# A convolutional LSTM ahead of an attention and experts block: the gates computed by one sigmoid, the skip split between ScalarE and GpSimd

## The chip, the cores and the metric

The kernel runs on one core of a Trainium2 chip. The metric is the device time of one execution in microseconds, by its median over the runs shown.

## The reference, cut to what matters

The input x is (16 samples, 96 channels, 16 rows, 16 columns). First comes a recurrent layer that walks over the 16 image rows, then an attention layer with six heads, then a feed-forward layer with four experts, all in float32. Only the recurrence is touched by the change. With the masked convolution of x shuffled into four gates of 48 channels, `h_rows`, it is:

```
def step(carry, h_row):
    _h, c = carry
    s = conv1d(_h, w1, width 3, padded) + h_row
    o, f, i, g = jnp.split(jax.nn.sigmoid(s), 4, axis=1)
    c = f * c + i * g
    _h = o * jnp.tanh(c)
    return ((_h, c), _h)
_, out_h = lax.scan(step, init, h_rows)
return x + conv1x1(out_h, w_skip * mask) + b_skip
```

Here `init` is zero, the convolution over `_h` runs along the 16 columns of a row, and the result, read as 256 tokens of 96 channels per sample, goes into the attention.

## The kernel before, in words

**Engines.** The program is written engine by engine, each with an order of its own, joined by semaphores. TensorE multiplies, VectorE (DVE), ScalarE (ACT) and GpSimd (POOL) compute, SyncE (SP) issues most transfers.

**Recurrence.** A row of the image is done in two half-steps, one for samples 0 to 7 and one for samples 8 to 15, so there are 32 half-steps m, each of 128 columns (8 samples by 16 positions). Half-step m depends on half-step m − 2. The four gates stand in one PSUM bank as two column blocks c = 0, 1 on 112 partitions: one gate of a block on partitions 0 to 47, the other on 64 to 111. Before: o and f in block 0, i and g in block 1. Four banks rotate as G[q].

In the order of one half-step: `input_part` (L857) puts the masked convolution of x into the bank, four matmuls over 96 partitions, two half-steps ahead. `state_part` (L870) adds the three taps over h: `wsa_sb` contracts over 112 partitions, since `h_pad` holds h on partitions 0 to 47 and once more, shifted by one column, on 64 to 111; `wsb_sb` adds the last tap. `skip` (L880) multiplies the h of half-step m − 2 with the skip weights into bank K. A 128-column float32 matmul is two records in the trace, each with its own weight load.

ACT takes tanh of half the gates (L466 for f and g, L467 for o and i), since sigmoid(x) = (1 + tanh(x/2))/2. VectorE works with these doubled values: `cell` (L620) with five instructions (L623 to L631), `cell_h` (L633) with the two writes of h (L641, L642), `add_skip` (L644) with one (L649) that adds skip, bias and x into `t_cm`. The factors 1/2 are put into the weights once, at L599 to L601. ACT's third instruction of a half-step is the tanh of c (L471). TensorE waits for h (`h_ready`), for a free bank (`gates_tanh`) and for the skip's bank (`t_half`). GpSimd has no work in this part but to clear buffers.

**Start.** SP issues w_input, the first two rows of x, w_state, two more rows, b_skip, the rest of x, then the other weights. VectorE waits for w_input (L594) and masks it (L596); TensorE then does four input parts. VectorE waits for w_state and b_skip (L598).

**End of the recurrence and what follows.** The last two skips wait for the last h; `keep_clock` (L909) issues small matmuls that nobody reads between the waits. With all of `t_cm` written (`t_half` = 32), TensorE transposes the first tokens (L928). Eight blocks of 512 tokens follow: layer norm, q, k and v, scores (L968 to L973), exponentials on ACT (L518) with the division on GpSimd (L406), transposes of the probabilities (L984), values (L1005, four or three matmuls with 32 output columns each, at different column groups), the output projection (L1011), the experts' first layer (L1042 to L1046) with Gelu, the routing (L753 is its last step on VectorE) and the experts' second layer (L1022, which adds the bias by a matmul with two contraction rows, then L1026).

## Time and profile before

| | us |
|---|---|
| median of 3 runs | 467.11 (464.62 to 467.35) |
| profiled execution, its own time | 466.77 |
| its span, first to last instruction | 465.0 |
| TensorE matmuls busy | 435.8 (94%) |
| VectorE busy | 269.5 (58%) |
| ScalarE busy | 263.6 (57%) |
| GpSimd busy | 145.8 (31%) |

The span is the profiled execution from its first to its last instruction; its own time holds what lies around that too. Busy time of TensorE is an upper figure, because matmuls are pipelined and their ends are modelled: the distance between the starts of two matmuls is the better measure of what one costs. In a timeline row, "x8" is eight records merged, the second number is the time that they span, and square brackets hold the idle time of the engine before them and what ended it.

### The profile page before, as it was taken

Reading aid. Unit: us, or ns where it says so; the run is one execution under the profiler, and the core shown is the slowest. Engines: PE = TensorE matmul, PEld = TensorE weight load, DVE = VectorE, ACT = ScalarE, POOL = GpSimd, SP = SyncE. Lnnn points to the kernel's source line nnn. Section 1 sums busy time; section 2 is a strip of 40 time slices with the busy share of each in tenths; the row PEclk is TensorE's granted clock in tenths of the full one; section 3 lists DMA queues with packets and bytes.
Section 4 is the critical chain, followed back from the end, with each engine's and each line's share of the span. In section 5 each row is a group of like instructions: output and inputs, shape, how many; then the busy total and the mean of one; then the engine's idle time right before and its main releaser. Section 6 shows DMA issues by size and latency. Waiting matters only on the chain.

```text
span 465.0 us, 10797 instructions
## 1 busy us (share of the span) xinstructions
PE 435.8 (94%) x3199; PEld 347.0 (75%) x3199; DVE 269.5 (58%) x954; ACT 263.6 (57%) x740; POOL 145.8 (31%) x309
## 2 busy tenths in 40 slices
PE   6999998759899999999999999999999999999897
PEld 6999996436568777877777778678767877787676
DVE  3888888535525852775277437634763585266424
ACT  2544454336477648664865585567657764865370
POOL 5000000425422542362255315531542254235200
PEclk9999999997999999999999999999999999999999
DMA  8600000021021002101210120022002100200000
GB/s 200 134 0 0 0 0 1 25 68 27 1 61 28 19 15 67 39 0 37 52 30 0 45 51 22 0 51 51 17 0 59 42 0 13 68 22 1 15 4 18
DMA packets 14393, 14.95 MB, mean 32 GB/s; under 512 B 5426, under 2 KB 11412, under 8 KB 14372
## 3 DMA queue, kind: packets, MB, share of 16 engines
q1 hardware_dynamic: 14180, 14.30, 12.3%
q0 software_dynamic: 192, 0.39, 0.3%
q8 instruction: 10, 0.16, 0.1%
q14 instruction: 11, 0.09, 0.1%
HBM read 3.86 MB, written 1.57 MB: 12 GB/s over the span
## 4 chain that ended last, share of the span: by engine, by line
PE 74%; DVE 12%; ACT 5%; issue 5%; SPq 2%; DMA 1%; POOL 1%; DVEq 1%; ACTq 0%; POOLq 0%
PE F L1026 19%; PE T L984 9%; PE A L1005 8%; PE F L1042 4%; PE S L968 4%; PE F L1046 4%; PE F L1043 3%; PE S L970 3%; PE F L1022 3%; PE S L973 2%; DVE c L629 2%; DVE ig L627 2%; ACT tc_sb L471 2%; DVE pt_sb L457 1%; PE M L947 1%
## 5 line engine op out<-in xcount | busy, mean ns | idle before, releaser
L406 POOL TENSOR_SCALAR p_sb<-p_sb,rden 128x128 f32<-128x128 f32 (+1 forms) x192 | 79.3, 427 | 133.4 <-DVE rden L710 131.2
L1026 PE MATMUL F<-w_sb,hid 128*128 128x96 f32 x768 | 101.0, 276 | 0.0
L1026 PEld LDWEIGHTS F<-w_sb,hid 128*128 128x128 f32 x768 | 93.4, 192 | 5.9 <-issue 5.9
L518 ACT ACTIVATE p_sb<-S,nmax 128x128 f32<-128x128 f32 (+1 forms) x192 | 78.8, 425 | 17.4 <-DVE nmax L704 17.3
L704 DVE TENSOR_REDUCE nmax<-S 128x2 f32<-128x512 f32 (+1 forms) x80 | 50.7, 634 | 53.1 <-PE S L973 52.8
L457 ACT COPY pt_sb<-T 128x512 f32<-128x512 f32 (+1 forms) x48 | 26.4, 550 | 69.2 <-PE T L984 69.2
L564 ACT ACTIVATE hid<-F,b_sb 128x512 f32<-128x512 f32 x72 | 49.3, 686 | 8.2 <-PE F L1046 7.5
L1005 PE MATMUL A<-pt_sb,v_cur 128*32 128x128 f32 x576 | 44.2, 284 | 8.4 <-ACT pt_sb L457 4.5
L984 PE MATMUL T<-id_sb,p_sb 128*128 128x128 f32 x288 | 49.3, 290 | 1.4 <-POOL p_sb L406 1.4
L968 PE MATMUL S<-k_bd,q_st 96*128 96x384 f32 (+2 forms) x96 | 38.7, 410 | 4.8 <-DMA k_bd<-k_cur 3.8
L984 PEld LDWEIGHTS T<-id_sb,p_sb 128*128 128x128 f32 x288 | 30.9, 143 | 16.2 <-issue 14.1
L518 ACT ACTIVATION_READ_ACCUMULATOR p_sb<-S,nmax 128x1 f32 x192 | 40.0, 208 | 0.0
L1005 PEld LDWEIGHTS A<-pt_sb,v_cur 128*32 128x32 f32 x576 | 22.3, 109 | 20.2 <-ACT pt_sb L457 9.3
L779 DVE SCALAR_TENSOR_TENSOR y_sb<-F,gw,y_sb 128x96 f32<-128x96 f32 x96 | 30.5, 318 | 3.4
L970 PE MATMUL S<-k_bd,q_st 96*128 96x384 f32 (+2 forms) x96 | 32.4, 344 | 0.0
L1042 PE MATMUL F<-x2hi,w1hi 96*128 96x512 f32 x72 | 30.0, 417 | 1.4 <-ACT x2hi L559 0.8
L865 PE MATMUL F<-x_pad,win_sb 96*112 (+1 forms) x192 | 27.2, 291 | 4.4 <-DMA x_pad<-in_x 4.4
L457 DVE COPY pt_sb<-T 128x384 f32<-128x384 f32 (+1 forms) x32 | 20.0, 624 | 18.5 <-PE T L984 18.5
L471 ACT ACTIVATE tc_sb<-c 48x128 f32<-48x128 f32 x32 | 9.9, 309 | 35.2 <-DVE c L629 35.2
L1046 PE MATMUL F<-x2lo,w1hi 96*128 96x512 f32 x72 | 29.3, 407 | 0.0
L1043 PE MATMUL F<-x2hi,w1lo 96*128 96x512 f32 x72 | 28.4, 395 | 0.0
L865 PEld LDWEIGHTS F<-x_pad,win_sb 96*112 96x112 f32 x192 | 24.9, 193 | 4.3 <-DVE win_sb L596 4.3
(142 smaller groups left out, 793.8 us busy)
## 6 DMA issues: line engine op xcount, KB each, us to landing
k_bd<-k_cur SPq DMA_DIRECT2D x96, 32.0 KB, 2.0
q_st<-q_cur SPq DMA_DIRECT2D x28, 96.0 KB, 2.2
k_bd<-k_cur SPq DMA_DIRECT2D x96, 16.0 KB, 1.8
t_st<-t_cm SPq DMA_DIRECT2D x7, 192.0 KB, 2.4
out_y<-y_sb SPq DMA_DIRECT2D x7, 192.0 KB, 1.9
x_pad<-in_x SPq DMA_DIRECT2D x2, 612.0 KB, 9.0
w_sb<-in_w SPq DMA_DIRECT2D x1, 576.0 KB
hid<-in_w SPq DMA_DIRECT2D x1, 576.0 KB, 7.5
```

Source lines behind the costliest of these rows:

```text
L406: last = nc.gpsimd.tensor_scalar(p, p, rden[:, u % 3, i:i + 1], 1.0, ALU.mult, ALU.mult)
L457: copy(pt_sb[:, u % 2, 0:w], T[:, 0:w]).then_inc(pt_done, 1)
L518: last = nc.scalar.activation(p_sb[:, u % 3, i * nk:(i + 1) * nk], S[u % 2][:, i * nk:(i + 1) * nk], ACT.Exp, bias=nmax[:, u % 3, i:i + 1] ...
L564: nc.scalar.activation(hid[:, c, :], L1[c % 4][:], ACT.Gelu, bias=b1_sb[:, c:c + 1]).then_inc(gelu_done, 1)
L704: V.tensor_reduce(nmax[:, u % 3, 0:HG[t]], S[u % 2][:, 0:HG[t] * nk].rearrange("p (h k) -> p h k", k=nk), AX.X, ALU.max, negate=True).then ...
L865: last = mm(G[q][0:GATE_M, c * HC:(c + 1) * HC], wi_sb[:, tap, c], xr[:, bs, tap:tap + W], start=(c == 0 and tap == 0), stop=ready, skip_g ...
L968: mm(d, q_st[:, g, ts], k_bd[:, a, 0, g, i0:i1, 0:nk], start=(3 * g + i0 == h0), stop=False, skip_group_check=True)
L984: last = nc.tensor.transpose(T[:, i * TT:(i + 1) * TT], p_sb[:, u % 3, i * TT:(i + 1) * TT], id_sb[:])
L1005: last = mm(A[VW * (h % 3):VW * (h % 3) + VW, 0:TT], v, pt_sb[:, u % 2, c0:c0 + TT], start=(kt == 0 and h < 3), stop=(kt == t and h >= 3), ...
L1026: last = mm(dst[:, e * C:(e + 1) * C], hid[:, c, s * TT:(s + 1) * TT], w2_sb[:, c], start=False, stop=(c == NCH - 1), skip_group_check=True)
L1042: mm(dst, w1hi[:, cs], x2hi[:], start=True, stop=False)
L1046: mm(dst, w1hi[:, cs], x2lo[:], start=False, stop=True).then_inc(hid_ready, 1)
```

## The change

The gates are placed anew: g and f in block 0, i and o in block 1, each block with the one on partitions 0 to 47 first. So i and g lie on the low partitions and f and o on the high ones. ACT takes one sigmoid of all 112 partitions by 256 columns. VectorE computes with the true values: i·g, f·c and their sum, all written on partitions 64 to 111, then h twice. Placing the gates needs the weights' columns in another order; it is made by the loads, four for w_input and five for w_state in place of one each, of which ACT issues five.

On every engine the two half-steps of a row are done together: VectorE does the cells of both, then the h of both; ACT the two sigmoids, then tanh and skip of one half, tanh and skip of the other. ACT copies the skip with its bias into `t_cm`, and GpSimd adds x in place; `t_half` now counts GpSimd's additions. On TensorE the last tap (`tap_ahead`) contracts over the 48 low partitions only and so needs only the first write of h; the skip contracts over the 48 high partitions. The order of the matmuls of a row is in `step`.

```diff
-        t_ig = sb("t_ig", [FEAT, 2, 2, HC])
-        t_fg = sb("t_fg", [FEAT, 2, 2, HC])
-        g1 = sb("g1", [FEAT, 2, HC])
-        fc = sb("fc", [FEAT, 2, HC])
-        ig = sb("ig", [FEAT, 2, HC])
-        c4 = sb("c4", [FEAT, 2, HC])
-        c2 = sb("c2", [FEAT, 2, HC])
-        tc_sb = sb("tc_sb", [FEAT, 2, HC])
+
+        gate = sb("gate", [GATE_M, 2, 2, HC])
+        fc = sb("fc", [GATE_M, 2, HC])
+        ig = sb("ig", [GATE_M, 2, HC])
+        cell = sb("cell", [GATE_M, 2, HC])
+        tc_sb = sb("tc_sb", [GATE_M, 2, HC])
...
-        W_REC, W_QK, W_ALL = 4, 5, 10
+        W_REC, W_QK, W_ALL = 2, 3, 8
         N_WIN = 14
+        N_WREC = 6
...
+        def skip_out(row, hb):
+
+            return t_cm[:].rearrange("p (b t) -> p b t", t=ROWS * W)[:, hb * HALF:(hb + 1) * HALF, bass.ds(row * W, W)]
+
+
+        SWAPS = ((0, slice(FEAT, GATE_M), 0), (1, slice(0, 64), 1))
+        CROSS = ((0, slice(0, FEAT), 1, slice(64, GATE_M)), (1, slice(64, GATE_M), 0, slice(0, FEAT)))
...
-            sp.dma_start(win_sb[:], w_input).then_inc(w_input_in, 16)
+            gates_st = wst_sb[:, 0:4 * GATE_M].rearrange("p (k m) -> p k m", m=GATE_M)
+            gates_in = w_state[:, 0:4 * GATE_M].rearrange("p (k m) -> p k m", m=GATE_M)
+            for blk, cols, blk_from in SWAPS:
+                sp.dma_start(win_sb[:, blk::2, cols], w_input[:, blk_from::2, cols]).then_inc(w_input_in, 16)
             for i, (r0, r1) in enumerate(((0, 2), (2, 4), (4, 10), (10, ROWS))):
                 sp.dma_start(x_pad[:, r0 * row:r1 * row], x[:, r0 * row:r1 * row]).then_inc(x_in[i], 16)
                 if i == 0:
-                    sp.dma_start(wst_sb[:], w_state).then_inc(w_rec_in, 16)
+                    for blk, cols, blk_from in SWAPS:
+                        sp.dma_start(gates_st[:, blk::2, cols], gates_in[:, blk_from::2, cols]).then_inc(w_rec_in, 16)
...
+            def add_input(m, hb, row):
+
+                pool.wait_ge(skip_taken, m + 1)
+                dst = skip_out(row, hb)
+                nc.gpsimd.tensor_tensor(dst, dst, x_row(row)[:, hb * HALF:(hb + 1) * HALF, 1:], ALU.add
+                                        ).then_inc(t_half, 1)
+
+            for i in range(4):
+                pool.wait_ge(x_in[i], 16)
+            with pool.Fori(0, ROWS // 2) as it:
+                for q in range(4):
+                    add_input(4 * it + q, q % 2, 2 * it + q // 2)
...
+            for blk, cols, blk_from, cols_from in CROSS:
+                act.dma_start(win_sb[:, blk::2, cols], w_input[:, blk_from::2, cols_from]).then_inc(w_input_in, 16)
+            for blk, cols, blk_from, cols_from in CROSS:
+                act.dma_start(gates_st[:, blk::2, cols], gates_in[:, blk_from::2, cols_from]).then_inc(w_rec_in, 16)
+            act.dma_start(wst_sb[UP, 4 * GATE_M:], w_state[LOW, 4 * GATE_M:]).then_inc(w_rec_in, 16)
             def cell_gates(m, hb, src):
                 act.wait_ge(gates_ready, m + 1)
-                v = src[:, 0:2 * HC].rearrange("p (c n) -> p c n", c=2)
-                nc.scalar.activation(t_fg[:, hb], v[64:64 + FEAT], ACT.Tanh, scale=0.5).then_inc(gates_tanh, 1)
-                nc.scalar.activation(t_ig[:, hb], v[0:FEAT], ACT.Tanh, scale=0.5).then_inc(gates_tanh, 1)
+                nc.scalar.activation(gate[:, hb], src[0:GATE_M, 0:2 * HC].rearrange("p (c n) -> p c n", c=2), ACT.Sigmoid
+                                     ).then_inc(gates_done, 1)
             def cell_out(m, hb):
-                act.wait_ge(cell_dve, 5 * m + 4)
-                nc.scalar.activation(tc_sb[:, hb], c4[:, hb], ACT.Tanh, scale=0.25).then_inc(cell_tanh, 1)
-            def rec0(it):
-                for q in range(4):
-                    m = 4 * it + q
-                    cell_gates(m, q % 2, G[q])
-                    cell_out(m, q % 2)
-            rec0(0)
+                act.wait_ge(cell_dve, 3 * m + 3)
+                nc.scalar.activation(tc_sb[UP, hb], cell[UP, hb], ACT.Tanh).then_inc(cell_tanh, 1)
+            def take_skip(m, hb, row):
+                act.wait_ge(skip_ready, m + 1)
+                nc.scalar.activation(skip_out(row, hb), K[hb][0:C, 0:HC].rearrange("p (b w) -> p b w", w=W), ACT.Identity,
+                                     bias=bsk_sb[:, 0:1]).then_inc(skip_taken, 1)
+            def step(row, q, first=False):
+                for hb in range(2):
+                    cell_gates(2 * row + hb, hb, G[q + hb])
+                for hb in range(2):
+                    cell_out(2 * row + hb, hb)
+                    if not first:
+                        take_skip(2 * row - 2 + hb, hb, row - 1)
+            step(0, 0, first=True)
+            act.wait_ge(w_rec_in, 16 * N_WREC)
+            step(1, 2)
             with act.Fori(1, ROWS // 2) as it:
-                rec0(it)
+                step(2 * it, 0)
+                step(2 * it + 1, 2)
+            for hb in range(2):
+                take_skip(STEPS - 2 + hb, hb, ROWS - 1)
...
-            dve.wait_ge(w_input_in, 16)
+            dve.wait_ge(w_input_in, 16 * 4)
             setup_step(V.tensor_tensor(wi_sb[:, 1], wi_sb[:, 1], wim_sb[:], ALU.mult))
-            dve.wait_ge(w_rec_in, 16 * 2)
-            setup_step(V.tensor_scalar(wsa_sb[:], wsa_sb[:], 0.5, None, ALU.mult))
-            setup_step(V.tensor_scalar(wsb_sb[:], wsb_sb[:], 0.5, None, ALU.mult))
-            setup_step(V.scalar_tensor_tensor(wsk_sb[:], wsk_sb[:], 0.5, wskm_sb[:], ALU.mult, ALU.mult))
+            dve.wait_ge(w_rec_in, 16 * N_WREC)
+            setup_step(V.tensor_tensor(wsk_sb[UP], wsk_sb[UP], wskm_sb[UP], ALU.mult))
...
+            def new_cell(m, hb):
+                dve.wait_ge(gates_done, m + 1)
+                V.tensor_tensor(ig[UP, hb], gate[LOW, hb, 0], gate[LOW, hb, 1], ALU.mult).then_inc(cell_dve, 1)
+                V.tensor_tensor(fc[UP, hb], gate[UP, hb, 0], cell[UP, hb], ALU.mult).then_inc(cell_dve, 1)
+                dve.wait_ge(cell_dve, 3 * m + 2)
+                V.tensor_tensor(cell[UP, hb], fc[UP, hb], ig[UP, hb], ALU.add).then_inc(cell_dve, 1)
...
+            def new_h(m, hb, first=False):
                 dve.wait_ge(cell_tanh, m + 1)
                 if not first:
                     dve.wait_ge(skip_ready, m - 1)
+                o = gate[UP, hb, 1].rearrange("p (b w) -> p b w", w=W)
+                t = tc_sb[UP, hb].rearrange("p (b w) -> p b w", w=W)
                 bs = slice(hb * HALF, (hb + 1) * HALF)
+                V.tensor_tensor(h_pad[LOW, bs, 1:1 + W], o, t, ALU.mult).then_inc(h_ready, 1)
+                V.tensor_tensor(h_pad[UP, bs, 0:W], o, t, ALU.mult).then_inc(h_ready, 1)
+            def step(row, first=False):
+                for hb in range(2):
+                    new_cell(2 * row + hb, hb)
+                for hb in range(2):
+                    new_h(2 * row + hb, hb, first)
+            step(0, first=True)
+            with dve.Fori(1, ROWS) as row:
+                step(row)
...
+            def tap_ahead(m, q, c):
+                if c == 0:
+                    pe.wait_ge(h_ready, 2 * m - 3)
                 bs = slice(q % 2 * HALF, (q % 2 + 1) * HALF)
+                mm(G[q][0:GATE_M, c * HC:(c + 1) * HC], wsb_sb[LOW, c], h_pad[LOW, bs, 2:2 + W], start=False, stop=False,
+                   skip_group_check=True)
+            def other_taps(m, q):
                 pe.wait_ge(h_ready, 2 * m - 2)
+                bs = slice(q % 2 * HALF, (q % 2 + 1) * HALF)
                 for c in range(2):
+                    last = mm(G[q][0:GATE_M, c * HC:(c + 1) * HC], wsa_sb[:, c], h_pad[:, bs, 0:W], start=False, stop=True,
+                              skip_group_check=True)
                 last.then_inc(gates_ready, 1)
             def skip(m, hb, fresh=False):
                 bs = slice(hb * HALF, (hb + 1) * HALF)
                 if not fresh:
+                    pe.wait_ge(skip_taken, m - 1)
+                mm(K[hb][0:C, 0:HC], wsk_sb[UP], h_pad[UP, bs, 0:W], start=True, stop=True).then_inc(skip_ready, 1)
+            def step(row, q, fresh=False, more=True):
+                m = 2 * row
+                for c in range(2):
+                    tap_ahead(m, q, c)
+                other_taps(m, q)
+                tap_ahead(m + 1, q + 1, 0)
+                skip(m - 2, 0, fresh)
+                tap_ahead(m + 1, q + 1, 1)
+                other_taps(m + 1, q + 1)
+                skip(m - 1, 1, fresh)
                 if more:
+                    for hb in range(2):
+                        input_part(m + 2 + hb, (q + 2) % 4 + hb, row + 1)
...
+            step(1, 2, fresh=True)
             for i in (2, 3):
                 pe.wait_ge(x_in[i], 16)
             with pe.Fori(1, ROWS // 2 - 1) as it:
-                for q in range(4):
-                    half_step(4 * it + q, q, 2 * it + q // 2)
-            for m in range(STEPS - 4, STEPS):
-                half_step(m, m % 4, m // 2, more=m < STEPS - 2)
+                step(2 * it, 0)
+                step(2 * it + 1, 2)
+            step(ROWS - 2, 0)
+            step(ROWS - 1, 2, more=False)
```

## Rows read from the trace of the kernel before

**Rows 1.** Busy time by stage: us, PE, PEld, DVE, ACT, POOL, clock, DMA share, GB/s

```profile
10.90:74.58 63.68, 62.40 (x517) 57.44 (x515) 55.14 (x227) 30.80 (x87) 0.00 (x0) 1.00 0.13 26
...
80.33:465.00 384.67, 362.09 (x2623) 279.95 (x2623) 205.85 (x694) 227.74 (x642) 139.06 (x300) 0.99 0.11 29
```

**Rows 2.** Timeline of TensorE, first taps of half-steps 4, 5 and 30: start, us, instruction

```profile
14.83 0.38 PE L876 MATMUL F<-h_pad,wst_sb 112*112 112x128 f32 x2
...
16.80 0.39 PE L876 MATMUL F<-h_pad,wst_sb 112*112 112x128 f32 x2
...
72.37 0.47 PE L876 MATMUL F<-h_pad,wst_sb 112*112 112x128 f32 x2
```

**Rows 3.** Timeline of VectorE and ACT over one half-step period

```profile
38.29 0.28 DVE L641 SCALAR_TENSOR_TENSOR h_pad<-t_ig,tc_sb 48x128 f32<-48x128 f32 x1
38.60 0.29 DVE L642 SCALAR_TENSOR_TENSOR h_pad<-t_ig,tc_sb 48x128 f32<-48x128 f32 x1
...
40.15 0.31 ACT L471 ACTIVATE tc_sb<-c 48x128 f32<-48x128 f32 x1 [1.09 <-DVE c L629]
...
40.50 0.28 DVE L641 SCALAR_TENSOR_TENSOR h_pad<-t_ig,tc_sb 48x128 f32<-48x128 f32 x1
```

**Rows 4.** Timeline of ACT: one tanh over half of the gates of a half-step

```profile
12.38 0.38 ACT L467 ACTIVATE t_ig<-F 48x256 f32<-48x256 f32 x1
```

**Rows 5.** Additions on GpSimd, by line: shortest, median and longest in ns

```profile
L396 POOL TENSOR_TENSOR tb<-t,bp_sb x8: 987/1009/1016, 84.2 to 397.8; 128x384 f32<-128x384 f32 x8
...
L412 POOL TENSOR_TENSOR x1f<-x1hi,x1lo x8: 1262/1292/1292, 88.2 to 398.8; 96x512 f32<-96x512 f32 x8
```

**Rows 6.** Timeline of TensorE in block 1, around outputs of 32 columns and two-row L1022

```profile
152.70 0.58 PE L1026 MATMUL F<-w_sb,hid 128*128 128x96 f32 x4
153.21 0.63 PE L1005 MATMUL A<-pt_sb,v_cur 128*32 128x128 f32 x8
153.77 0.66 PE L984 MATMUL T<-id_sb,p_sb 128*128 128x128 f32 x4
154.26 0.36 PE L1011 MATMUL M<-wp_sb,o_t 96*128 96x96 f32 x2
...
154.66 0.33 PE L970 MATMUL S<-k_bd,q_st 96*128 96x384 f32 x1
154.84 0.34 PE L973 MATMUL S<-causal_sb,idb_sb 128*128 128x384 bf16 x1
155.10 0.44 PE L1022 MATMUL F<-b2hl,ones 2*128 2x384 f32 x1
155.47 0.91 PE L1026 MATMUL F<-w_sb,hid 128*128 128x96 f32 x6
156.31 0.63 PE L1005 MATMUL A<-pt_sb,v_cur 128*32 128x128 f32 x8
```

**Rows 7.** Timeline of TensorE and VectorE at the start of the kernel

```profile
4.36 5.43 PE L865 MATMUL F<-x_pad,win_sb 96*112 96x128 f32 x24 [4.36 <-DMA x_pad<-in_x]
...
3.65 0.39 DVE L596 TENSOR_TENSOR win_sb<-win_sb 96x224 f32<-96x224 f32 x1 [3.65 <-DMA win_sb<-in_w_input]
7.37 0.28 DVE L599 TENSOR_SCALAR wst_sb<-wst_sb 112x224 f32<-112x224 f32 x1 [3.34 <-DMA bsk_sb<-in_b_skip]
```

**Rows 8.** DMA in 11 to 13 us and in 3 to 5 us: packets, MB, share

```profile
q1 hardware_dynamic: 973, 0.37, 125.9%
...
q1 hardware_dynamic: 267, 0.52, 99.9%
```

**Rows 9.** Timeline of TensorE: the first transpose of t_cm

```profile
80.33 0.55 PE L928 MATMUL M<-id_sb,t_cm 96*128 96x96 f32 x4
```

**Rows 10.** ACT's table loads by line, and its first exponential in the timeline

```profile
L532 ACT ACT_TABLE_LOAD  x7: 1283/1283/1283, 141.5 to 406.7; - x7
...
97.58 0.37 ACT L518 ACTIVATE p_sb<-S,nmax 128x128 f32<-128x128 f32 x1 [5.39 <-DVE nmax L704]
```

**Rows 11.** L753 on VectorE by line, and GpSimd's timeline beside its first instance

```profile
L753 DVE TENSOR_TENSOR gw<-gkp,grd x8: 175/295/296, 145.1 to 453.1; 128x16 f32<-128x16 f32 x8
...
144.61 1.08 POOL L406 TENSOR_SCALAR p_sb<-p_sb,rden 128x128 f32<-128x128 f32 x3 [13.81 <-DVE rden L710]
```

More of the change, by code:

```diff
@@ L218, in hybrid_kernel @@
         h_ready = sem("h_ready")
+        skip_taken = sem("skip_taken")
         t_half = sem("t_half")
@@ L637, in cell_h @@
                     dve.wait_ge(skip_ready, m - 1)
-                o = t_ig[:, hb, 0].rearrange("p (b w) -> p b w", w=W)
-                t = tc_sb[:, hb].rearrange("p (b w) -> p b w", w=W)
+                o = gate[UP, hb, 1].rearrange("p (b w) -> p b w", w=W)
+                t = tc_sb[UP, hb].rearrange("p (b w) -> p b w", w=W)
                 bs = slice(hb * HALF, (hb + 1) * HALF)
-                V.scalar_tensor_tensor(h_pad[0:FEAT, bs, 1:1 + W], o, 1.0, t, ALU.add, ALU.mult).then_inc(h_ready, 1)
-                V.scalar_tensor_tensor(h_pad[64:64 + FEAT, bs, 0:W], o, 1.0, t, ALU.add, ALU.mult).then_inc(h_ready, 1)
-            def add_skip(m, hb, row):
-                dve.wait_ge(skip_ready, m + 1)
-                bs = slice(hb * HALF, (hb + 1) * HALF)
-                dst = t_cm[:].rearrange("p (b t) -> p b t", t=ROWS * W)[:, bs, bass.ds(row * W, W)]
-                V.scalar_tensor_tensor(dst, K[hb][0:C, 0:HC].rearrange("p (b w) -> p b w", w=W),
-                                       bsk_sb[:, 0:1], x_row(row)[:, bs, 1:], ALU.add, ALU.add).then_inc(t_half, 1)
-            def rec0(it, first):
-                for q in range(4):
-                    m, hb = 4 * it + q, q % 2
-                    cell(m, hb)
-                    cell_h(m, hb, first=first and q < 2)
-                    if q >= 2 or not first:
-                        add_skip(m - 2, hb, 2 * it + q // 2 - 1)
-            dve.wait_ge(x_in[0], 16)
-            rec0(0, True)
-            for i in (1, 2, 3):
-                dve.wait_ge(x_in[i], 16)
-            with dve.Fori(1, ROWS // 2) as it:
-                rec0(it, False)
-            for hb in range(2):
-                add_skip(STEPS - 2 + hb, hb, ROWS - 1)
+                V.tensor_tensor(h_pad[LOW, bs, 1:1 + W], o, t, ALU.mult).then_inc(h_ready, 1)
[8 more added lines that the diff above has]
+                step(row)
             split_qk_weights()
@@ L882, in skip @@
                 if not fresh:
-                    pe.wait_ge(t_half, m - 1)
-                mm(K[hb][0:C, 0:HC], wsk_sb[:], h_pad[:, bs, 1:1 + W], start=True, stop=True).then_inc(skip_ready, 1)
-            def half_step(m, q, row, fresh=False, more=True):
-                state_part(m, q)
-                skip(m - 2, q % 2, fresh)
+                    pe.wait_ge(skip_taken, m - 1)
[10 more added lines that the diff above has]
+                skip(m - 1, 1, fresh)
                 if more:
-                    input_part(m + 2, (q + 2) % 4, row + 1)
+                    for hb in range(2):
+                        input_part(m + 2 + hb, (q + 2) % 4 + hb, row + 1)
             pe.wait_ge(w_dve, 1)
@@ L899, in _ @@
             pe.wait_ge(x_in[1], 16)
-            for m in (2, 3):
-                half_step(m, m, m // 2, fresh=True)
+            step(1, 2, fresh=True)
             for i in (2, 3):
@@ L904, in _ @@
             with pe.Fori(1, ROWS // 2 - 1) as it:
-                for q in range(4):
-                    half_step(4 * it + q, q, 2 * it + q // 2)
-            for m in range(STEPS - 4, STEPS):
-                half_step(m, m % 4, m // 2, more=m < STEPS - 2)
+                step(2 * it, 0)
+                step(2 * it + 1, 2)
+            step(ROWS - 2, 0)
+            step(ROWS - 1, 2, more=False)
             def keep_clock(count):
```

27 lines of the change are left out of this document (7 added, 20 removed).

## The prediction

> **What bounds the kernel now.** I first read the table by stage [rows 1]. The recurrence is the stretch from 10.90 to 80.33 us. The eight token blocks behind it take 384.67 us, are not edited, and start when the first transpose of t_cm can run (TensorE, 80.33 us). So only the time of that transpose counts, as long as the later blocks keep their pace. In the recurrence all engines but one are nearly full by that table: PE 62.4 of 63.68 us, DVE 55.1, ACT 30.8, POOL nothing. Busy PE is not proof, so the second view is the timeline. A half-step's matmuls, issued back to back, repeat after 16.80 − 14.83 = 1.97 us [rows 2]; later the period is 40.50 − 38.29 = 2.21 us [rows 3]. From half-step 2 (10.90, the edge of the stage in [rows 1]) to half-step 30 (72.37) it is 61.47 us for 14 rows of the image, **4.39 us a row**, against 2 x 1.97 = 3.94 us that TensorE needs [rows 2]. The third view is the timeline of VectorE and ACT [rows 3]: VectorE is busy 87% of the stage, its eight instructions stand one behind the other, and ACT waits 1.09 us of each period for its result c. So VectorE is the bound, by 0.45 us a row over TensorE, and that 0.45 us is all that a lighter VectorE can win: 14 x 0.45 = 6.3 us, or 1.3% of the time.
>
> **The change, part by part, over one row (two half-steps).**
>
> *VectorE.* Out go g1, the two factors and the skip addition. What remains is ig, fc, cell and two h writes per half, ten instructions. Their price is in [rows 3]: 0.31 us from L641's start to L642's, which writes at other partitions, the dearest case there. At most 10 x 0.31 = 3.1 us, under 3.94: VectorE stops being the bound. Its setup steps at L599 to L601 shrink to one.
>
> *ACT.* One sigmoid of 112x256 takes the place of two tanh of 48x256. Its 256 columns are those of L467, which takes 0.38 us [rows 4]; with the handover to the next I count 0.41. Two tanh at 0.34 and two copies of the skip at 0.31 (L471) to 0.37 us (L518, with a bias) are added: 2.2 us a row, hidden.
>
> *POOL.* Two additions of 96x128 a row. 384 columns take 0.99 us and 512 take 1.26 [rows 5], so about 0.44 us for 128, hidden unless VectorE is stopped by it (below).
>
> *TensorE.* The count of matmuls stays, but six of the 18 a row now contract over 48 partitions: the four of tap_ahead (partitions 0 to 47) and the two of skip (64 to 111). They stand in three places: ahead of the taps of half A, around the skip of A, and after the taps of half B. The trace does not show a contraction over 48. Above it, 96 next to 112 costs nothing: L865 and L876 keep the pace of 0.109 us a record [rows 2]. Below it, switching costs. L970 and L973, with 384 columns each, show it: L970 holds TensorE for 0.18 us (154.66 to 154.84), L973, with the two-row L1022 behind it, for 0.26, and L1022 itself, 384 columns too, for 0.37 [rows 6], and the six L1026 behind it take 0.84 us (to L1005 at 156.31) instead of 6 x 0.11 = 0.66, of which I give half to the exit from L1022 and half to the entry to L1005. So this visit costs 0.08 + 0.19 + 0.09 = 0.36 us. A visit to outputs of 32 columns (L1005) is priced in the same rows: 152.70 to 154.26 is 1.56 us for 4 + 8 + 4 records; with the eight running two at a time the pace gives 12 x 0.109 = 1.30. So it costs 0.26 us, and neighbours on different parts of the array overlap (alone they would take 16 x 0.109 = 1.74). For 48 rows I take the cost as there, because less than half of the array is used, and of the two prices 0.26, because L1005 is a 128-column f32 matmul in two records like ours. Ends: 0 and 0.36. Three visits: +0.78. For the skip between the two tap_ahead I take one matmul (two records, 0.22 us) as overlapped; ends 0 and 0.22. A row is then 3.94 + 0.78 − 0.22 = **4.50 us**, ends 3.72 and 5.02; over 14 rows +1.5 us against 4.39, ends −9.4 and +8.8. The Trainium skill, page "TensorEngine Tiling (Array Packing)", sections Tiling Modes, Key Properties, says that contractions up to 64 rows get tiles of their own and that a change of tiling mode drains the engine; no row here shows 48. By it the cost cannot be 0.
>
> *Does the other chain still fit?* With a row's first matmul at 0, half A's gates come out at 0.10 + 0.44 + 0.15 + 0.44 + 0.2 = 1.33 us, half B's at 2.46; B's sigmoid ends at 2.87, VectorE does ig, fc and cell of B to 3.80 and has written the low h of A by 4.08 us. TensorE asks for it at 4.50: hidden, with 0.4 us to spare.
>
> *Start.* TensorE starts at 4.36 us, after w_input (landed 3.65) and the first x [rows 7]. The new w_input, now in four DMAs, comes in 96 x 12 runs of 192 or 256 bytes. Small packets cost 1.259 x 32 us / 973 = 41 ns of an engine, those of 1.9 KB 120 ns [rows 8]: 1152 x 41 / 16 = 3.0 us in place of 1.0. w_state, by the same sum, takes 2.4 in place of 1.1, on a second queue that runs beside the first x. SP issues one DMA more ahead of x (0.46 us), ACT five of its own, done by 3.1 us, with its table load 4.4: before the gates come. Ends: +0.5 (only the issue) and +3.8 us (2.0 + 1.3 + 0.5); I take **+1.6**, half of the two excesses, since two queues share the work and the first x needs only a part of it. VectorE's side (bsk_sb landed 7.37, now some 9.9, then 2.3 us to the first h) ends at 12.2, under 10.90 + 1.6 = 12.5.
>
> *End of the recurrence.* Before, half-step 30 to the transpose is 80.33 − 72.37 = 7.96 us [rows 2, 9]. New: the last h at 5.0, keep_clock's eight matmuls to 6.15, skip 0.5, ACT 0.37, POOL 0.44: about 7.6. **−0.4 us** (ends −1.2 and +0.5). ACT and POOL stand one after the other here, where VectorE was alone.
>
> *Table.* Exp has the table that tanh used, since no load stands before L518. After sigmoids it needs one (1.28 us, as at L532), which falls into ACT's idle 5.39 us [rows 10]: 0.
>
> **Sum:** 1.6 + 1.5 − 0.4 = +2.7 us on the profiled execution's 466.77 us, which lies 0.34 under the median: 469.8 by the median of 467.11. One per cent, what a measurement tells from nothing, is 4.67 us: 462.4 to 471.8.
>
> **Rivals.**
> 1. *Switching to 48 rows is free.* Then a row is TensorE's 3.94 us or, with the overlap, held by the chain of h at about 3.9: −6.3, start +1.6, end −1.2: −5.9, so **461.2 us**. For it: 96 rows cost nothing, and adjacent small matmuls overlapped. Against: both kinds of small tile in [rows 6] cost. The skill, page "TensorE: Matmul & The Clock Gate", Part 3, says that matmuls in different row groups start about 4 ns apart; by that the overlap is full, which the three switches still outweigh.
> 2. *Slower: POOL holds VectorE at the low h of A.* POOL's addition comes right after ACT's copy of the skip, while VectorE, now always with two SBUF inputs, is at cell and h. Such a VectorE instruction was held by POOL: L753 takes 0.295 us where POOL's L406 runs beside it, seven times of eight, and 0.175 in the last block, where POOL has ended [rows 11]. The addition begins after cell of B (3.8), ends at 4.2, and h follows at 4.4 to 4.5; above 4.50 minus TensorE's weight load (0.1) it decides. Each further 0.3 us a row, with B's h behind a second addition, is +4.2: 2.7 + 4.2, so **474.0 us**. Against: one addition just fits into the 0.4 us to spare.
> 3. *Sigmoid and tanh reload a table each row:* 16 x 2 x 1.28 = 41 us, **511 us**. ACT's rows cannot exclude it. The skill, page "ScalarE: Activation LUTs", Table sets, lists tanh in sigmoid's set; by it there is no reload.
>
> **Chances.** Forecast 0.61 (own range 465 to 478), rival 1 0.24, rival 2 0.13, rival 3 0.02. Of the forecast 0.38 lies within 1% and 0.23 above; rival 1 gives 0.18 faster and 0.06 within; rival 2 0.01 within, 0.12 slower; rival 3 slower. Together faster 0.18, within 0.45, slower 0.37. Range 461 to 477: it takes in rival 1's time and rival 2's, and leaves out rival 3, the top of the forecast's own range and half of what rival 1 might give beyond its figure.
>
> **What would show it.** Period of a row on TensorE: 4.5 (3.9 in rival 1, 4.8 in rival 2). Gaps at the first tap_ahead, the first other tap and the skip of B, 0.1 to 0.2 us each over 0.109 (right), or none (rival 1). PE never waiting for h_pad in the loop (right), or waiting, with h_pad records of 0.4 us beside POOL's (rival 2). First matmul at about 6.0 us, half-step 2 at 12.5, first transpose of t_cm at 83. ACT_TABLE_LOAD one more, before L518's successor. What would make it wrong: a start bound by w_state far later than 9.9 us, or other blocks' pace changing with TensorE's clock, which no term here covers.

## The result: 1.5% slower, and where the time went

The changed kernel takes **473.03 us** (median of 4 runs, 472.62 to 474.15) against 465.88 us (4 runs, 464.62 to 467.35) for the kernel before on the same chip: ratio **1.0149, 95% interval 1.0124 to 1.0173**. Its profiled execution spans 472.6 us, against 465.0 before. The prediction was made from three of the four runs of the kernel before, with the median 467.11.

First the table by stage, as in [rows 1] (us, then busy time of PE, PEld, DVE, ACT, POOL, clock, DMA share, GB/s). The first stage is 14 rows of the image, from the first tap ahead of half-step 2 to that of half-step 30; the second begins at the first transpose of `t_cm`.

```profile
12.64:79.74 67.10, 67.10 (x505) 55.87 (x504) 43.21 (x139) 29.47 (x84) 13.25 (x27) 1.00 0.09 22
87.83:472.60 384.77, 362.28 (x2623) 280.43 (x2623) 206.13 (x694) 228.75 (x643) 138.94 (x300) 0.99 0.11 29
```

TensorE is busy in all 67.10 us, and VectorE has dropped from 87% of its stage to 64%: the bound has moved to TensorE, as intended. But 67.10 us is more than the 61.47 us that VectorE needed. The four terms, each against its stretch before:

- start (0 to half-step 2): 12.64 − 10.90 = **+1.74 us**
- 14 rows: 67.10 − 61.47 = **+5.63 us** (a row 4.79 against 4.39)
- end (half-step 30 to the transpose): 8.09 − 7.96 = **+0.13 us**
- the eight blocks: 384.77 − 384.67 = **+0.10 us**

They add to 7.60 us, the difference of the spans. The start is the least certain of them. Of the kernels of the experiments below, e1 has the same start and e2 nearly the same, and they reach half-step 2 at 11.60 and 12.06 us. e6 and e3, whose start is that of the kernel before, reach it at 10.15 and 11.56. The first matmul varies less: 5.88 to 6.19 us with the new start, 4.36 to 4.73 with the old. Next, TensorE's timeline over one row (start, us, engine, line, what, records). The start of each line to the start of the next is what counts, since the ends are modelled.

```profile
41.40 0.69 PE L902 MATMUL F<-h_pad,wst_sb 48*112 48x128 f32 x4
42.01 0.69 PE L910 MATMUL F<-h_pad,wst_sb 112*112 112x128 f32 x4
42.63 0.36 PE L902 MATMUL A<-h_pad,wst_sb 48*112 48x128 f32 x1
42.64 0.46 PE L918 MATMUL M<-h_pad,wst_sb 48*96 48x128 f32 x2
42.84 0.49 PE L902 MATMUL A<-h_pad,wst_sb 48*112 48x128 f32 x3
43.25 0.69 PE L910 MATMUL A<-h_pad,wst_sb 112*112 112x128 f32 x4
43.87 0.46 PE L918 MATMUL T<-h_pad,wst_sb 48*96 48x128 f32 x2
44.26 2.00 PE L892 MATMUL F<-x_pad,win_sb 96*112 x16
46.19 0.47 PE L902 MATMUL F<-h_pad,wst_sb 48*112 48x128 f32 x2
```

At the pace of 0.109 us a record, four records are 0.44, two 0.22 and sixteen 1.74. Here they take 0.61, 0.62, 0.62 (this one with the skip's two records besides), 0.62, 0.39 and 1.93. Every time that TensorE goes from 48 rows to 112 or 96, or back, about **0.18 us** is lost: six times a row, 1.08 us. The skip between the taps ahead costs nothing (its 0.22 us is saved). So a row is 3.93 (36 records at the pace) + 1.08 − 0.22 = 4.79 us. TensorE waits for no h in the loop. What the others do at the same time:

```profile
40.24 0.29 DVE L672 TENSOR_TENSOR cell<-fc,ig 48x128 f32<-48x128 f32 x1
40.56 0.29 DVE L682 TENSOR_TENSOR h_pad<-gate,tc_sb 48x128 f32<-48x128 f32 x1
40.56 0.58 POOL L454 TENSOR_TENSOR t_cm<-t_cm,x_pad  x1 [3.45 <-ACT t_cm L510]
40.88 0.42 DVE L683 TENSOR_TENSOR h_pad<-gate,tc_sb 48x128 f32<-48x128 f32 x1
...
42.74 0.38 ACT L499 ACTIVATE gate<-F 112x256 f32<-112x256 f32 x1 [1.48 <-PE F L910]
```

The low copy of A's h (L682) is there at 40.85 us, 0.55 us before the taps at 41.40 want it. The second copy takes 0.42 us behind the start of GpSimd's addition where the first takes 0.29. ACT waits 1.48 us for TensorE's gates: it was VectorE's c that it waited for before [rows 3].

The start, against [rows 7] (SPq is the time that the queue takes to issue):

```profile
0.73 1.64 SPq L311 DMA_DIRECT2D win_sb<-in_w_input  x2
...
2.41 0.61 SPq L313 DMA_DIRECT2D x_pad<-in_x  x1
...
3.80 1.28 ACT L499 ACT_TABLE_LOAD   x1 [3.80 <-issue]
...
5.24 0.39 DVE L644 TENSOR_TENSOR win_sb<-win_sb 96x224 f32<-96x224 f32 x1 [5.24 <-DMA win_sb<-in_w_input]
...
6.19 2.02 PE L892 MATMUL F<-x_pad,win_sb 96*112 96x128 f32 x8 [6.19 <-DMA x_pad<-in_x]
...
7.56 0.26 DVE L647 TENSOR_TENSOR wst_sb<-wst_sb 48x96 f32<-48x96 f32 x1 [1.93 <-DMA bsk_sb<-in_b_skip]
```

SP takes 0.82 us to issue each of the two transfers in small pieces, so the first x is asked for at 2.41 us, 1.22 later than before (1.19); it lands at 6.19, where 4.36 us was the start of TensorE before [rows 7]. Of these 1.83 us, then, 1.22 pass before x is asked for and 0.61 on its way. The input weights are in at 5.24 us, earlier than x.

And the end, against [rows 9]:

```profile
84.49 0.46 PE L918 MATMUL M<-h_pad,wst_sb 48*96 48x128 f32 x2 [0.73 <-DVE h_pad L683]
84.78 0.42 DVE L683 TENSOR_TENSOR h_pad<-gate,tc_sb 48x128 f32<-48x128 f32 x1
84.88 1.47 PE L953 MATMUL F<-causal_sb,idb_sb 128*128 128x384 bf16 x8
...
86.28 0.46 PE L918 MATMUL T<-h_pad,wst_sb 48*96 48x128 f32 x2
...
87.83 0.55 PE L969 MATMUL M<-id_sb,t_cm 96*128 96x96 f32 x4 [0.66 <-POOL t_cm L454]
```

B's last h is written at 85.20 us, and its skip starts at 86.28, behind the eight matmuls of `keep_clock` (L953).

### The profile page after: what moved, and what is told of

Same layout as the page of the kernel before. It is cut to its first block, busy times and chain, and to the rows that moved or that the text cites. A ratio compares the mean times of both kernels' runs of the same rounds, so it can differ in the third digit from the quotient of the medians.

```text
span 472.6 us, 10775 instructions
## 1 busy us (share of the span) xinstructions
PE 442.5 (94%) x3199; PEld 346.6 (73%) x3199; DVE 257.0 (54%) x856; ACT 264.1 (56%) x741; POOL 161.2 (34%) x341
## 4 chain that ended last, share of the span: by engine, by line
PE 87%; DVE 4%; ACT 3%; SPq 2%; issue 2%; POOL 1%; DMA 1%; POOLq 0%; DVEq 0%; ACTq 0%
PE F L1067 19%; PE T L1025 8%; PE A L1046 8%; PE F L892 6%; PE F L1083 4%; PE F L1087 4%; PE S L1009 3%; PE F L1084 3%; PE S L1011 3%; PE F L910 3%; PE F L902 3%; PE F L1063 2%; PE S L1014 2%; PE A L892 2%; DVE pt_sb L483 1%
## 5 line engine op out<-in xcount | busy, mean ns | idle before, releaser
L1067 PE MATMUL F<-w_sb,hid 128*128 128x96 f32 x768 | 102.3, 278 | 0.0
L1067 PEld LDWEIGHTS F<-w_sb,hid 128*128 128x128 f32 x768 | 94.7, 194 | 6.0 <-issue 6.0
L566 ACT ACTIVATE p_sb<-S,nmax 128x128 f32<-128x128 f32 (+1 forms) x192 | 78.7, 424 | 15.6 <-DVE nmax L731 15.4
L1009 PE MATMUL S<-k_bd,q_st 96*128 96x384 f32 (+2 forms) x96 | 37.8, 401 | 4.2 <-DMA k_bd<-k_cur 3.3
L566 ACT ACTIVATION_READ_ACCUMULATOR p_sb<-S,nmax 128x1 f32 x192 | 39.9, 208 | 0.0
L454 POOL TENSOR_TENSOR t_cm<-t_cm,x_pad x32 | 15.5, 484 | 65.0 <-ACT t_cm L510 65.0
L1011 PE MATMUL S<-k_bd,q_st 96*128 96x384 f32 (+2 forms) x96 | 31.7, 338 | 0.0
```

The lines of the kernel that those rows point to most:

```text
L566: last = nc.scalar.activation(p_sb[:, u % 3, i * nk:(i + 1) * nk], S[u % 2][:, i * nk:(i + 1) * nk], ACT.Exp, bias=nmax[:, u % 3, i:i + 1] ...
L1009: mm(d, q_st[:, g, ts], k_bd[:, a, 0, g, i0:i1, 0:nk], start=(3 * g + i0 == h0), stop=False, skip_group_check=True)
L1067: last = mm(dst[:, e * C:(e + 1) * C], hid[:, c, s * TT:(s + 1) * TT], w2_sb[:, c], start=False, stop=(c == NCH - 1), skip_group_check=True)
```

## Experiments

The theory after the result: what costs is the change between a contraction of 48 rows and one of more, 0.18 us each way. Rivals: it is the small matmuls themselves; it is the place or the waits; it is the chain over VectorE and GpSimd. In the table, "row" is the period of a row in the profile, "tokens" the first transpose of `t_cm`; the interval is that of the ratio to the kernel before.

| kernel | row, us | tokens, us | median, us | ratio (interval) |
|---|---|---|---|---|
| before | 4.39 | 80.33 | 465.88 to 466.70 by comparison | 1 |
| after | 4.79 | 87.83 | 473.03 | 1.0149 (1.0124 to 1.0173) |
| e1_skip_apart | 5.01 | 89.85 | 475.83 | 1.021 (1.0159 to 1.0261) |
| e2_full_height | 4.42 | 81.37 | 466.27 | 1.0003 (0.9976 to 1.003) |
| e3_before_skip48 | 4.64 | 83.65 | 468.93 | 1.0069 (1.0034 to 1.0104) |
| e4_before_skip65 | 4.39 | 80.37 | 466.73 | 1.0002 (0.9972 to 1.0032) |
| e5_host_layout | 4.79 | 86.38 | 471.33 | 1.0102 (1.0068 to 1.0135) |
| e6_before_skip64 | 4.64 | 82.30 | 469.48 | 1.0076 (1.0046 to 1.0106) |
| e7_full_host_order | 4.29 | 78.13 | 463.49 | 0.994 (0.9918 to 0.9962) |
| e8_full_host_keep2 | 4.28 | 77.20 | 462.35 | 0.9924 (0.9895 to 0.9952) |
| e9_two_visits | 4.30 | 78.61 | 464.35 | 0.9968 (0.9951 to 0.9985) |
| e10_add_after_h | 4.17 | 75.04 | 461.07 | 0.9909 (0.9885 to 0.9933) |
| e11_add_at_end | 4.17 | 88.81 | 477.0 (one run) | – |

### The skip away from the taps ahead

```diff
                 tap_ahead(m + 1, q + 1, 0)
-                skip(m - 2, 0, fresh)
                 tap_ahead(m + 1, q + 1, 1)
                 other_taps(m + 1, q + 1)
+                skip(m - 2, 0, fresh)
                 skip(m - 1, 1, fresh)
```

> The changed kernel with the skip of half A moved from between the two tap_ahead of half B to just ahead of the skip of half B; same matmuls, same three visits to 48-row contractions. Theory T (each visit costs 0.36 us and the skip between the two tap_ahead is overlapped, 0.22 us): the row goes from 4.79 to 5.01 us, the kernel 3 us slower than the changed one, about 476. Rival W (TensorE's row is set by waiting for h, not by the tiles): row unchanged at 4.79, same time. Rival N (visits cost less and nothing is overlapped): row unchanged as well.

The two skips, one behind the other:

```profile
44.15 0.46 PE L918 MATMUL M<-h_pad,wst_sb 48*96 48x128 f32 x2
44.44 0.38 PE L918 MATMUL T<-h_pad,wst_sb 48*96 48x128 f32 x2
44.75 0.91 PE L892 MATMUL F<-x_pad,win_sb 96*112 x6
```

They take 0.60 us where the second alone took 0.39. The row is 5.01 us, 0.22 more: two neighbours at 48 rows on different rows of the array share their time, and the skip alone pays for its two records. The medians differ by 2.8 us, where 14 x 0.22 = 3.1 was expected. The profiled execution alone, 473.92 us, would have hidden it: its first taps came 1.04 us earlier (11.60), and its blocks, the same code, ran in 382.45 us, 2.3 us less than after the change. Here the row is the safer reading.

### The same work over all 112 rows

```diff
-                mm(G[q][0:GATE_M, c * HC:(c + 1) * HC], wsb_sb[LOW, c], h_pad[LOW, bs, 2:2 + W], start=False, stop=False,
+                mm(G[q][0:GATE_M, c * HC:(c + 1) * HC], wsb_sb[:, c], h_pad[:, bs, 2:2 + W], start=False, stop=False,
...
-                mm(K[hb][0:C, 0:HC], wsk_sb[UP], h_pad[UP, bs, 0:W], start=True, stop=True).then_inc(skip_ready, 1)
+                mm(K[hb][0:C, 0:HC], wsk_sb[:], h_pad[:, bs, 0:W], start=True, stop=True).then_inc(skip_ready, 1)
```

> The changed kernel with the last tap and the skip contracted over all 112 partitions (the added weight rows are zero), so no 48-row contraction is left; each last tap now waits for both writes of h. Order of the matmuls as in the changed kernel. Theory T: TensorE needs 3.94 us a row, then the chain over the second write of h decides, about 4.3 us (h of A written at 4.26 after the row's start): 14 x (4.79 - 4.3) = 6.9 us faster than the changed kernel, about 466. Rival W: the taps wait longer than before the edit, the row grows by the 0.3 us of the second write, about 477.

The edit also makes the last taps wait for both copies of h, since they now read all 112 rows. Seven microseconds come back, with more rows multiplied. Timeline of all engines but the weight loads, at the first taps of a row:

```profile
42.17 0.29 DVE L682 TENSOR_TENSOR h_pad<-gate,tc_sb 48x128 f32<-48x128 f32 x1
42.25 0.50 POOL L454 TENSOR_TENSOR t_cm<-t_cm,x_pad  x1 [3.15 <-ACT t_cm L510]
42.49 0.41 DVE L683 TENSOR_TENSOR h_pad<-gate,tc_sb 48x128 f32<-48x128 f32 x1
...
42.96 0.69 PE L902 MATMUL F<-h_pad,wst_sb 112*112 112x128 f32 x4 [0.23 <-DVE h_pad L683]
43.49 0.60 PE L910 MATMUL F<-h_pad,wst_sb 112*112 112x128 f32 x4
43.92 0.38 PE L902 MATMUL F<-h_pad,wst_sb 112*112 112x128 f32 x2
```

From L910 to L902 the pace is 0.109 us a record; the first four records take 0.53 in place of 0.44, but they stand behind a wait. The first taps of the kernel before are longer in the same way with no change of rows (0.31 for two in place of 0.22, at 72.37 us). Now TensorE waits 0.23 us for the second copy of h: the chain over VectorE is the bound, at 4.42 us, and GpSimd's addition stands beside the write that ends it.

### The kernel before with its skip over 48, 64 and 65 rows

The kernel before, with one number changed in the skip. Rows 48 to 63 hold nothing and row 64 begins the second copy, whose weights are zero there, so these compute the same.

```diff
-                mm(K[hb][0:C, 0:HC], wsk_sb[:], h_pad[:, bs, 1:1 + W], start=True, stop=True).then_inc(skip_ready, 1)
+                mm(K[hb][0:C, 0:HC], wsk_sb[0:48], h_pad[0:48, bs, 1:1 + W], start=True, stop=True).then_inc(skip_ready, 1)
```

> The kernel before with one edit: its skip contracts over the 48 partitions that have weights, not over 112. One visit a half-step, no overlap possible. Theory T: TensorE needs 1.97 + 0.36 = 2.33 us a half-step and takes over from VectorE's 2.20: row 4.39 to 4.66, 3.8 us slower than before. At the price of my forecast (0.26) 2.23 us, 0.4 to 1 us slower. Rival F (a 48-row contraction is free): same as before.

> The kernel before with its skip over 65 partitions in place of 112. If it is the array's division at 64 rows that costs, 65 rows cost nothing and the time is that of before. If any contraction much narrower than its neighbours costs, 3.8 us slower, like the one over 48.

> The kernel before, its skip multiplied over the first 64 rows of h and weights (outputs as in the reference: rows 48 to 63 hold nothing of h and have no weight). Theory T (an operand of at most 64 rows works in a smaller tile of the array, and changing between tilings costs about 0.18 us each way): as with 48 rows, half-step 2.32 us and 468.9 us. Theory U (the cost comes with rows not a multiple of 32 or with partial quadrants, so 48 and not 64): half-step 2.19 us, 466.5 us.

TensorE's timelines, first with 48 rows, then with 64, then with 65:

```profile
40.05 0.38 PE L877 MATMUL F<-h_pad,wst_sb 112*112 112x128 f32 x2
40.36 0.46 PE L884 MATMUL M<-h_pad,wst_sb 48*96 48x128 f32 x2
40.74 1.13 PE L865 MATMUL F<-x_pad,win_sb 96*112 x8
41.71 0.38 PE L876 MATMUL A<-h_pad,wst_sb 112*112 112x128 f32 x2
```

```profile
41.01 0.38 PE L877 MATMUL A<-h_pad,wst_sb 112*112 112x128 f32 x2
41.32 0.46 PE L884 MATMUL T<-h_pad,wst_sb 64*96 64x128 f32 x2
41.71 1.13 PE L865 MATMUL F<-x_pad,win_sb 96*112 x8
```

```profile
41.94 0.38 PE L877 MATMUL F<-h_pad,wst_sb 112*112 112x128 f32 x2
42.16 0.38 PE L884 MATMUL M<-h_pad,wst_sb 65*96 65x128 f32 x2
42.38 0.60 PE L865 MATMUL F<-x_pad,win_sb 96*112 x4
```

With 48 rows, L877 to L884 is 0.31 us (0.22 for two records), L884 to L865 0.38 (0.22), and the eight inputs 0.97 (0.87): a lone visit costs 0.09 + 0.16 + 0.10 = **0.35 us**. With 64 it is 0.31 and 0.39, and the half-step again 2.32 us. With 65 it is 0.22 and 0.22: nothing. The times agree: ratios of 1.0069 and 1.0076 with 48 and 64 rows, 1.0002 with 65. So it is not the number of rows, nor 48 being no multiple of 32, but on which side of 64 the operand lies. The Trainium skill, "TensorEngine Tiling (Array Packing)", Tiling Modes, gives operands of up to 64 rows a tile of their own, and its Key Properties say that a change of mode drains the engine. The boundary is where the page has it, and each change across it costs 0.18 us here, on the way in and on the way out, as a drain would; the drain itself is in no row of the profile.

### The weights reordered by the host

The input parameters of the kernel are laid out in the new order of the gates, so that two whole transfers take the place of nine in pieces. The first of the edits:

```diff
-            for blk, cols, blk_from in SWAPS:
-                sp.dma_start(win_sb[:, blk::2, cols], w_input[:, blk_from::2, cols]).then_inc(w_input_in, 16)
+            sp.dma_start(win_sb[:], w_input).then_inc(w_input_in, 16)
```

> The changed kernel, with the sigmoid's order of the gate weights written by the host: two whole transfers on SyncE's queue as before, none on ScalarE's, no split into pieces. The row on TensorE is as after the change. Theory D (the start's 1.8 us are the reordering transfers: SyncE issues L311's two in 1.64 us and L313 two more, and VectorE gets the last input weights at 5.24 us): first matmul at 4.4 us, half-step 2 at 10.9 to 11.2, row 4.79, 471.3 us. Theory S (the start is longer because of the steps themselves, the whole-tile sigmoid and its chain): half-step 2 stays at 12.6 less at most 0.3, 472.8 us.

The first matmul is at 4.58 us, the first tap ahead at 11.19, the tokens 1.45 us earlier, the time 1.7 us less. The start's loss is the transfers, nearly all of it, by the first matmul (6.19 to 4.58 us, where 4.36 to 4.73 was the kernel before). The times alone would not show it: the two intervals overlap.

### All rows, reordered weights, the skips last; and a shorter keep_clock

The edits of e2 and e5, and the skip of A moved as in e1. The second kernel differs from the first in one number:

```diff
-                keep_clock((6, 8)[hb])
+                keep_clock((6, 2)[hb])
```

> Taps and skip over all 112 rows (the rest of the weights zero), host-written order of the weights, and both skips after the taps of B, so that B's gates end one skip (0.22 us) earlier. In the full-height kernel the row was 4.42 us: VectorE wrote h of A after the new cell of B, the taps of A waited 0.23 us for it. Theory C (that chain, taps A to taps B to sigmoid B to cell B to h of A, sets the row): the row is 4.42 - 0.22 = 4.20 us, half-step 2 at 11.0, 466.3 - 1.7 - 3.1 = 461.5 us. Theory P (TensorE's own work sets it from here): row 3.94 us, 458 us. Theory N (the place of the skip is nothing): row 4.42, 464.6 us.

> As e7_full_host_order, with two in place of eight matmuls that keep the clock between the two last skips. After the change the last skip waited for those eight, from h at 85.2 us to 86.28. If the wait for them is on the path to the tokens, the tokens come 0.9 to 1.1 us earlier and the time is 1 us below e7_full_host_order, about 460.5 us. If the granted clock falls for the want of them, the first block takes it back: the stretch after the tokens grows by as much or more, 461.5 to 463 us.

The row fell to 4.29, not 4.20, and the time to 463.49, not 461.5. VectorE's timeline of e7 says why:

```profile
42.33 0.28 DVE L662 TENSOR_TENSOR ig<-gate 48x128 f32<-48x128 f32 x1 [0.87 <-ACT gate L492]
...
42.97 0.29 DVE L665 TENSOR_TENSOR cell<-fc,ig 48x128 f32<-48x128 f32 x1
43.29 0.28 DVE L662 TENSOR_TENSOR ig<-gate 48x128 f32<-48x128 f32 x1
...
44.25 0.29 DVE L675 TENSOR_TENSOR h_pad<-gate,tc_sb 48x128 f32<-48x128 f32 x1
```

B's sigmoid came earlier (0.87 us behind A's in place of 1.10), but VectorE went from A's cell to B's ig without a pause: with A's gates on, eight instructions stand one behind the other until both copies of A's h are written. The chain begins at A's gates, not B's. The expectation followed the wrong one of the two, by 0.09 us a row.

With two matmuls in place of eight between the last skips, the tokens come 0.93 us earlier and the time falls by 1.1 us. Of the 0.93, 0.76 lies behind the first of the two last skips (75.06 to 78.13 us in e7, 74.89 to 77.20 in e8); the rest came before the edited place. The blocks take 383.17 and 383.00 us and the granted clock is 0.992 in both profiles, so nothing was taken back: the last skip did wait for matmuls whose result nobody reads.

### Two visits in place of three

The second skip moves behind the inputs, next to the following row's taps ahead, in the kernel of e5.

```diff
                 other_taps(m + 1, q + 1)
-                skip(m - 1, 1, fresh)
                 if more:
                     for hb in range(2):
                         input_part(m + 2 + hb, (q + 2) % 4 + hb, row + 1)
+                skip(m - 1, 1, fresh)
```

> The changed kernel with host-written order of the weights (e5_host_layout), its second skip moved behind the input's matmuls, next to the next row's first taps ahead. Both work in tiles of at most 64 rows, so a row has two visits to the small tile in place of three, and both skips stand beside taps ahead of the other rows. Theory T (each visit costs 0.36 us, a neighbouring pair overlaps for 0.22): row = 3.92 + 2 x 0.36 - 2 x 0.22 = 4.20 us, against 4.79 in e5_host_layout; 471.3 - 14 x 0.59 = 463.1 us. Theory C (the chain over VectorE sets a floor, as in the full-height kernel, 4.29 us, and h's low copy of B now waits for the late skip): row 4.3 to 4.5, 464.5 to 467 us. Theory V (what costs is each instruction with fewer rows, 0.09 us apiece, not the visit): 4.79 - 0.22 = 4.57 us, 468.3 us.

```profile
40.33 0.35 PE L911 MATMUL T<-h_pad,wst_sb 48*96 48x128 f32 x1
...
40.41 0.36 PE L895 MATMUL F<-h_pad,wst_sb 48*112 48x128 f32 x1
...
44.37 0.29 DVE L675 TENSOR_TENSOR h_pad<-gate,tc_sb 48x128 f32<-48x128 f32 x1
...
44.64 0.35 PE L911 MATMUL T<-h_pad,wst_sb 48*96 48x128 f32 x1
```

The row is 4.30 (40.33 to 44.64 is 4.31), 0.49 less than with three visits where the count of switches and overlaps gave 0.59. The price by the instruction (theory V, 4.57) is out. Of the last tenth 0.07 is theory C's: the taps beside the skip start at 44.71, 0.07 behind it, since they wait for the low copy of h that VectorE writes from 44.37 to 44.66.

### GpSimd's additions moved away from the writes of h

```diff
                 pool.wait_ge(skip_taken, m + 1)
+                if hb == 0 and not last:
+                    pool.wait_ge(h_ready, 4 * row + 6)
```

> As e8_full_host_keep2, with GpSimd's add of A's x held back until VectorE has written both copies of A's h in that row (one wait on GpSimd; work unchanged). In e7 and e8 the row is 4.29 us and the taps of A wait for the second copy of h, which takes 0.41 us beside GpSimd's add where the first takes 0.29. Theory H (the two engines' two-input operations hold each other up): A's second copy takes 0.29 us, the row 4.17 us, 14 x 0.12 = 1.7 us less: 460.7 us; the writes of B's h take 0.41 instead, within their slack of 0.26 us. Theory W (the second copy is longer for another cause, its place or the upper rows): it stays 0.41 us, row 4.29, 462.4 us.

And as a bound, the same kernel (e8) with all additions behind the recurrence:

```diff
+            pool.wait_ge(skip_taken, STEPS)
             with pool.Fori(0, ROWS // 2) as it:
```

> As e8_full_host_keep2, but GpSimd starts no add of x until the last skip is taken: no GpSimd work beside the recurrence, all 32 adds behind it. Theory H: both copies of h take 0.29 us in every half and the row is 4.17 us, as in e10_add_after_h; the adds, 32 x 0.44 = 14 us, then stand ahead of the tokens, so about 474 us. Theory W: the second copy is 0.41 us still and the row 4.29 us.

In e10, B's second copy beside an addition, and in the next row the two writes of A's h, with no addition beside them; then A's second copy in e11:

```profile
39.84 0.43 POOL L454 TENSOR_TENSOR t_cm<-t_cm,x_pad  x1 [3.36 <-DVE h_pad L679]
39.85 0.57 DVE L680 TENSOR_TENSOR h_pad<-gate,tc_sb 48x128 f32<-48x128 f32 x1
...
43.05 0.29 DVE L679 TENSOR_TENSOR h_pad<-gate,tc_sb 48x128 f32<-48x128 f32 x1
...
43.37 0.29 DVE L680 TENSOR_TENSOR h_pad<-gate,tc_sb 48x128 f32<-48x128 f32 x1
...
43.72 0.69 PE L899 MATMUL F<-h_pad,wst_sb 112*112 112x128 f32 x4
```

```profile
44.01 0.29 DVE L677 TENSOR_TENSOR h_pad<-gate,tc_sb 48x128 f32<-48x128 f32 x1
```

Without GpSimd beside them the second copies take 0.29 us, like the first; B's, which begins 0.01 us after an addition, takes 0.57. TensorE's taps of A (L899) follow the second copy at once. The row is 4.17 us in both kernels, as forecast. So the two engines do hold each other, 0.12 us of A's second copy, and on the path that was worth 14 x 0.12 = 1.7 us; measured from e8 to e10 it was 1.3 us by the medians. Their intervals overlap (0.9895 to 0.9952 and 0.9885 to 0.9933), so it is the row, 4.28 to 4.17, that shows it.

e11 gave 477.0, not 474. Its 32 additions took 13.08 us, and TensorE stood idle for 13.9. The blocks behind them took 386.4 us against 383.0 in e8; their first 2.2 us ran at a granted clock of 0.50, the lower of the two levels, where the first 2.8 us of e8's ran at 1.00.

**e10 has the lowest median of this study**: 461.07 us, 0.9% under the kernel before and 12 us under the change as it was made. It keeps the change's sigmoid and its split over ACT and GpSimd. It drops the 48-row operands and the transfers in pieces, and it moves the skip of A, shortens `keep_clock` and holds back GpSimd. The shorter `keep_clock` was not tried in the kernel before, so what the sigmoid and the split alone are worth against it is not shown; the row, 4.39 to 4.17, is the part that `keep_clock` does not touch.

## Why the prediction was right in the direction and short by 4.9 us

Forecast +2.7 us on the profiled execution, measured +7.6; in medians 469.8 against 473.03, inside the range of 461 to 477. That range is wide because it was drawn around both rivals, so lying in it says little for the sum. Point by point:

- **The bound moves from VectorE to TensorE, 0.45 us a row is the most to win:** right. VectorE is busy 64% of the rows' stretch, and TensorE waits for nothing in it. The sentence that calls all engines but one nearly full misreads its table, where ACT is busy 30.8 of 63.68 us; nothing in the sum rests on it.
- **The price of a visit to 48 rows: this is the step that failed.** The prediction had two prices, 0.26 us from outputs of 32 columns (L1005) and 0.36 from the two-row contraction (L1022) [rows 6], and took 0.26 because L1005 is a 128-column float32 matmul like ours. Measured: six changes of 0.18, so 0.36 a visit, and 0.35 for a lone visit in e3. The nearer row was the one that, like ours, cuts the *contraction*. That its 0.36 fits to the hundredth is partly luck: a half of the loss behind L1022 was given to it by assumption. Three visits x 0.10 x 14 rows = 4.2 us; the 14 rows came out 4.1 us over the forecast (4.79 against 4.50), of the 4.9 us missing. e2, e3, e4 and e6 show that what costs is the boundary at 64 rows.
- **The overlap of the skip, 0.22 us:** right; e1 takes it away and the row grows by 0.22.
- **The chain of h has 0.4 us to spare:** right, 0.55 us, though in part because the row is longer: the low copy of A is written 4.25 us after the row's first tap (at 36.60), where 4.08 was forecast. Over 112 rows the chain decides, at 4.42 us (e2), because the taps then wait for the second copy as well.
- **Rival 1 (switching is free):** out, by the visits' price. Its 3.9 us for the chain was sound: in e2 the low copy, all that a 48-row tap needs, is written 3.92 us after the row's first tap (42.46 against 38.54).
- **Start +1.6:** +1.74, and that closeness is luck: with that start e1 and e2 reach half-step 2 only 0.70 and 1.16 us after the kernel before. Its mechanism was half right: it is the transfers in pieces (e5), but mostly through the issue on SP (0.82 us each, where the prediction counted 0.46 for the added one), which put x back by 1.22 us of 1.83, and less through the time on the way. w_rec was ready at 7.56 us, not 9.9: `b_skip` came earlier than the sum of packets had it, and it never mattered.
- **End −0.4:** +0.13. The order was as told, each link later: B's last h 5.46 us after half-step 30's first tap (5.0 forecast; the two visits ahead of it at 0.10 more each and 0.13 of a second copy held by GpSimd are 0.33 of the 0.46, the rest is not traced), `keep_clock` to 6.54 (6.15), and 1.55 us for skip, ACT and GpSimd with the waits between them (1.45). e8 shows that `keep_clock` is in the path: 0.76 us.
- **Table reload hidden:** right. One more load (L566, 1.28 us at 100.54) with 0.0 us of idle time ahead of it, and ACT then waits 4.02 us for VectorE. No load stands in the recurrence: one at 3.80 us, before the first sigmoid. Rival 3 is out.
- **Rival 2 (GpSimd holds VectorE at A's h):** the mechanism is there, at the second copy and not the low one, and costs nothing in the rows after the change because TensorE is later still. The low copy begins before the addition or with it, and then takes 0.29 us. Rival 2 was priced at 0.3 us a row; it is 0.12 (e10, e11), and counts only where TensorE waits for the second copy. The 4.79 us row that the prediction named as rival 2's sign came from another cause, and only the wait of TensorE for h_pad, which is absent, told the two apart.
- **The blocks keep their pace:** +0.10 us after the change. It is not a constant of the code, though: 382.4 us (e9, mean granted clock of the execution 0.999) to 385.9 us (e3, 0.988), e11 left aside.

## What to carry over

Before splitting an operand to save rows, count how often TensorE would go across 64 rows of contraction and back, and charge 0.18 us each time (128-column float32 matmuls). Zero weights over the full height cost TensorE nothing, but the operand's other rows must then be written first, which in e2 was a wait of 0.23 us a row. Small matmuls that must be are put side by side so that they share a visit and overlap. When two rows of a trace could price an unknown step, take the one that shares its mechanism (what is cut: the contraction or the outputs), not the one with the same shape of operand. And when the bound moves off an engine, work out the next chain in its full order on that engine, and look at who touches the same buffers beside its last link.
